# Four graph layers on one core: scores from upper and lower operand parts, and a layer norm folded into the product behind it

## The reference, cut to what matters

```python
# L0: two hypergraph convolutions with relu and a layer norm between them
h = relu(hypergraph_conv(x, adj, W1, b1))          # conv(x) = Dn * H @ (Be * (H.T @ (x @ W.T))) + b, H = (adj != 0)
h = layer_norm(h, gamma, beta)                     # (h - mu) * rsqrt(var + eps) * gamma + beta, over 512 channels
y = hypergraph_conv(h, adj, W2, b2) + x
# L1: transition matrix from exp(leaky_relu(si + sj)) * A, row-normed, then two hops
H = sum(Xk @ Wk[k] + bk[k] for k in range(3));  Xk = transition @ Xk     # out = relu(H)
# L2: eight heads of 32 channels
Xp = X @ Wp[h] + bp[h];  Xc = Xp @ C[h].T
attn = tanh(A * (Xc @ Xp.T));  Xh = attn @ Xp      # out = relu(Xh)
# L3
out = relu((a @ x) @ kernel) * mask
```

## Time and profile before

| | |
|---|---|
| median of 3 runs | 1648.58 us (1648.41 to 1649.86) |
| the profiled execution | 1649.85 us, its span 1648.0 us |
| TensorE busy | 1486.1 us (90%), 9850 products |
| VectorE, ScalarE, GpSimd busy | 1146.0 us (70%), 908.8 us (55%), 284.7 us (17%) |
| mean granted TensorE clock | 0.978 of full |

### The profile page before, as it was taken

How to read it: one execution, slowest core, us unless ns; L and a number is a source line. 1 busy time by engine, 2 the same in 40 slices (tenths; PEclk the granted TensorE clock), 3 DMA queues, 4 the chain that set the end, 5 groups by cost and what they waited for, 6 DMA issues and landing times.

```text
span 1648.0 us, 26778 instructions
## 1 busy us (share of the span) xinstructions
PE 1486.1 (90%) x9850; PEld 1085.8 (66%) x9850; DVE 1146.0 (70%) x2522; ACT 908.8 (55%) x1517; POOL 284.7 (17%) x348
## 2 busy tenths in 40 slices
PE   5688888899899999999999999999999999998986
PEld 4676666667666676766667676666767666676633
DVE  6564766758678686777868677786867778676663
ACT  3424555365565546556554655656465565646564
POOL 3111020202112030210303021030302103120001
PEclk9788999999999999999999999999999999999998
DMA  7010111112120211212021121202112121110021
...
DMA packets 58550, 92.17 MB, mean 56 GB/s; under 512 B 4288, under 2 KB 23296, under 8 KB 58496
## 3 DMA queue, kind: packets, MB, share of 16 engines
...
...
## 4 chain that ended last, share of the span: by engine, by line
PE 55%; issue 20%; DVE 16%; ACT 6%; POOL 2%; DMA 1%; SPq 0%; DVEq 0%; ACTq 0%; POOLq 0%
PE ring_f L1299 33%; PE ring_b L1299 9%; PE ring_b L1569 6%; PE pv_acc L1585 3%; DVE att L1133 3%; DVE bns L928 3%; PE ring_f L1468 2%; POOL rstd L489 2%; DVE rows L1030 2%; ACT hf L568 1%; DVE uz L952 1%; ACT rows L606 1%; DVE m L957 1%; DVE xc_s L952 1%; PE ring_f L1435 1%
## 5 line engine op out<-in xcount | busy, mean ns | idle before, releaser
L1133 DVE TENSOR_TENSOR att<-ring_b,at 128x1024 f32<-128x1024 f32 x256 | 307.2, 1219 | 77.1 <-PE ring_b L1569 69.7
L710 ACT ACTIVATE att<-att 128x1024 f32<-128x1024 f32 x256 | 265.1, 1054 | 136.2 <-DVE att L1133 135.2
L489 POOL TENSOR_TENSOR rstd<-var,mhalf 128x4 f32<-128x4 f32 x80 | 81.3, 1017 | 769.6 <-DVE var L943 769.6
L1299 PE MATMUL ring_f<-w,uz 128*128 128x256 f32 (+1 forms) x896 | 188.9, 333 | 2.3 <-DVE uz L952 1.7
L1299 PE MATMUL ring_f<-m,tr_h 128*128 128x256 f32 x1024 | 190.4, 287 | 0.0
L1299 PEld LDWEIGHTS ring_f<-m,tr_h 128*128 128x128 f32 x1024 | 158.9, 191 | 32.8 <-issue 32.1
L1299 PEld LDWEIGHTS ring_f<-w,uz 128*128 128x128 f32 x896 | 152.0, 192 | 29.8 <-DVE uz L952 12.2
L1585 PE MATMUL pv_acc<-att,xp_n 128*32 128x512 f32 x1024 | 138.5, 617 | 33.9 <-ACT att L710 26.8
L1569 PE MATMUL ring_b<-xc_t,xp_t 32*128 32x512 f32 x1024 | 147.6, 646 | 20.9 <-DVE att L1133 11.7
L1299 PE MATMUL ring_f<-m,inc_n 128*128 128x256 f32 x1024 | 132.2, 288 | 17.8 <-POOL m L493 16.3
L1299 PEld LDWEIGHTS ring_f<-m,inc_n 128*128 128x128 f32 x1024 | 127.0, 195 | 30.6 <-issue 18.7
...
## 6 DMA issues: line engine op xcount, KB each, us to landing
...
```

The lines of the kernel that those rows point to most:

```text
L489: pool.tensor_tensor(rstd[k][:], var[k][:], mhalf[:], ALU.pow).then_inc(rstd_made[k].sem, 1)
L710: act.activation(v, v, ACT.Tanh).then_inc(tanh_made.sem, 1)
L1133: dve.tensor_tensor(att[:, u % 2, 2 * half:2 * half + 2], ring_b[half][:], at[:, u % NT].unsqueeze(1).broadcast_to([P, 2, N]), ALU.mult).t ...
L1299: ins = pe.matmul(dst, lhsT, rhs, start=(first and n == 0), stop=(last and n == len(pairs) - 1), skip_group_check=True)
```

## The change

Five things, and new order lists on all five queues.

- Scores: `xp_t` and `xc_t` are each kept as an upper and a lower `fp32r` part. The new step `k_split` makes xp's (two operations of VectorE on 1024 columns), a new `k_xc` on VectorE xc's lower part. `k_scores` issues three rounds of four heads.
- The norm of z: `f_z` and its offset are gone. `f_zT` transposes the relu's output. `f_xw` scales rows by rstd on its way out of PSUM (`scaled`, `scaled_low` with `rstd[Z]`), and the mean and beta come in through a six-row product of `stat_t[0:6]` with `rowz[0:6]`, issued with the last part of `f_xw` instead of the first.
- The new step `f_stat` makes those six rows: five small operations on VectorE, four transposes of six columns into a ring bank, one copy on ScalarE.
- To make room, `xp_t` now lies in `hb`, and `xc_s` (with `ax_s`) in `tr_l`. `k_h2` waits for `xc_full`, `xn_full` and `xp_split` of the graph before, `f_tt` for `xp_full` and `o_full`.
- Set-up makes `rowz` instead of the first row of `rowb`.

```diff
-        xp_t = sb("xp_t", [P, 2, N])
-        xc_t = sb("xc_t", [P, 2, N])
-        xc_s = sb("xc_s", [P, 2, 2 * N], F32R)
+        xp_t = hb[:].rearrange("p t d -> p (t d)").rearrange("p (c n) -> p c n", c=2)
+        xp_s = sb("xp_s", [P, 2, 2, N], F32R)
+        xc_t = sb("xc_t", [P, 2, 2, N], F32R)
+        xc_s = tr_l[:].rearrange("p t n -> p (t n)").rearrange("p (a n) -> p a n", a=2)
...
-            def f_z(g, i):
-                if i == 0 and not seen(g, 1):
-                    set_up_w2()
-                normed(g, rows, rows, Z, i, ACT.Identity)
+            def f_stat(g):
+                act.wait_ge(stat_full.sem, stat_full.after(g, 1))
...
+                copy(stat_t[0:6], bank_of(ST, 0)[0:6], stat_copied)
...
-                copy(m1[:, 0, 2 * k:2 * k + 2].rearrange("p t d -> p (t d)"), bank_of(XW, k)[:], xw_hi)
+                scaled(k, bank_of(XW, k), rstd[Z], lambda t: m1[:, 0, t], xw_hi)
...
+            def f_stat(g):
+
+                cols = stat[:].rearrange("p t (a k) -> p a t k", a=2)
+                dve.wait_ge(rstd_made[Z].sem, rstd_made[Z].after(g, 1))
...
+                dve.tensor_scalar(pair[:, 0], sums[Z][:, :, 0], -0.5, None, ALU.mult)
+                c_stat.link(dve.tensor_tensor(pair[:, 1], var[Z][:], rstd[Z][:], ALU.mult))
+                here(c_stat, g)
+                dve.tensor_copy(cols[:, :, :, 0], pair[:])
+                c_stat.link(dve.tensor_copy(cols[:, :, :, 1], pair[:]))
+                here(c_stat, g)
+                dve.tensor_tensor(cols[:, :, :, 2], pair[:], cols[:, :, :, 0].bitcast(F32), ALU.subtract)\
+                   .then_inc(stat_made.sem, 1)
...
-                low(v[:, 1], bank_of(XW, k)[:], v[:, 0], xw_lo)
+                scaled_low(k, bank_of(XW, k), rstd[Z], lambda t: m1[:, 1, t], lambda t: m1[:, 0, t], xw_lo)
...
+            def k_split(g, part):
+                if part == 0:
...
+                    dve.wait_ge(xp_made.sem, xp_made.after(g, 2))
+                    dve.tensor_copy(xp_s[:, 0], xp_t).then_inc(xp_split.sem, 1)
+                else:
+                    dve.wait_ge(xp_split.sem, xp_split.after(g, 1))
+                    low(xp_s[:, 1], xp_t, xp_s[:, 0], xp_split)
+
+            def k_xc(g):
+                dve.wait_ge(xc_made.sem, xc_made.after(g, 1))
+                low(xc_t[:, 1], ring_b[0][:], xc_t[:, 0], xc_lo)
...
-                        pe.wait_ge(h_made[Z].sem, h_made[Z].after(g, i + 1))
+                        pe.wait_ge(relu_made.sem, relu_made.after(g, i + 1))
...
-                    pairs = [(sel[:], rowb[:, 0])] if ks[0] == 0 else []
+                    pairs = [(stat_t[0:6, i * P:(i + 1) * P], rowz[0:6])] if ks[-1] == HT_ - 1 else []
...
+            def f_stat(g):
+                pe.wait_ge(stat_made.sem, stat_made.after(g, 1))
+                ps = bank(g, ST, 0)
+                for i in range(NT):
+                    ins = pe.transpose(ps[0:6, i * P:(i + 1) * P], stat[:, i].bitcast(F32), ident[:])
+                ins.then_inc(stat_full.sem, 1)
...
-                for h in range(4):
-                    head = slice(h * KH, (h + 1) * KH)
-                    ins = pe.matmul(ring_b[h // 2][:, h % 2], xp_t[head, part, t * P:(t + 1) * P], xc_t[head, part],
-                                    start=True, stop=True, skip_group_check=True)
-                    if h % 2 == 1:
-                        ins.then_inc(scored.sem, 1)
+                for n, (p, c) in enumerate(((0, 0), (0, 1), (1, 0))):
+                    for h in range(4):
+                        head = slice(h * KH, (h + 1) * KH)
+                        ins = pe.matmul(ring_b[h // 2][:, h % 2], xp_s[head, p, part, t * P:(t + 1) * P],
+                                        xc_t[head, c, part], start=(n == 0), stop=(n == 2), skip_group_check=True)
+                        if n == 2 and h % 2 == 1:
+                            ins.then_inc(scored.sem, 1)
```

The lists of `turn`, for SP, TensorE and the part of VectorE's that the prediction speaks of (ScalarE's and GpSimd's are reordered in the same way):

```diff
 SP
-                    (0, next_x), (2, next_at), (0, next_wrow), (4, store), (2, next_at2), (0, next_adj),
+                    (0, next_x), (2, next_at), (4, store), (3, next_at2), (0, next_adj), (0, next_wrow),
                     (0, next_adjt),
 TensorE
-                    (0, f_m, 0), (0, f_m, 1), (2, k_attend, 2), (2, k_scores, 4), (0, f_u, 0), (0, f_u, 1),
-                    (2, k_attend, 3), (2, k_scores, 5), (0, f_conv1, 0), (0, f_conv1, 1), (0, f_conv1, 2),
-                    (0, f_conv1, 3), (2, k_attend, 4), (2, k_scores, 6), (2, k_attend, 5), (2, k_scores, 7),
-                    (0, f_zT, 0), (0, f_zT, 1), (1, k_hT), (0, f_zT, 2), (0, f_zT, 3), (0, f_xw, 0), (0, f_xw, 1),
-                    (0, f_xw, 2), (0, f_xw, 3), (2, k_attend, 6), (0, f_m2, 0), (0, f_m2, 1), (2, k_outT, 0),
-                    (2, k_attend, 7), (0, f_y, 0), (2, k_outT, 1), (0, f_y, 1), (1, k_xp, 0), (1, k_xp, 1),
-                    (1, k_xn, 0), (1, k_xc, 0), (0, f_hT, 0), (0, f_hT, 1), (1, k_xc, 1), (1, k_xn, 1), (0, f_sj),
-                    (0, f_q, 0), (0, f_q, 1), (2, k_ax, 0, 0), (0, f_q, 2), (0, f_q, 3), (2, k_ax, 0, 1),
-                    (2, k_ax, 1, 0), (2, k_ax, 1, 1), (2, k_out, 0), (2, k_out, 1), (0, f_tt, 0), (0, f_tt, 1),
-                    (0, f_tt, 2), (1, k_scores, 0), (0, f_tt, 3), (0, f_r1), (1, k_scores, 1), (0, f_r, 0),
-                    (1, k_attend, 0), (0, f_r, 1), (1, k_scores, 2), (0, f_x1), (1, k_attend, 1), (1, k_scores, 3),
-                    (0, f_x2, 0), (0, f_x2, 1),
+                    (0, f_m, 0), (2, k_scores, 3), (1, f_x2, 1), (2, k_attend, 2), (0, f_m, 1), (2, k_scores, 4),
+                    (0, f_u, 0), (2, k_attend, 3), (0, f_u, 1), (2, k_scores, 5), (0, f_conv1, 0), (0, f_conv1, 1),
+                    (0, f_conv1, 2), (0, f_conv1, 3), (2, k_attend, 4), (2, k_scores, 6), (0, f_zT, 0),
+                    (0, f_zT, 1), (2, k_attend, 5), (0, f_zT, 2), (0, f_zT, 3), (0, f_xw, 0), (0, f_xw, 1),
+                    (0, f_stat), (2, k_scores, 7), (0, f_xw, 2), (0, f_xw, 3), (2, k_attend, 6), (0, f_m2, 0),
+                    (0, f_m2, 1), (1, k_hT), (2, k_outT, 0), (0, f_y, 0), (2, k_attend, 7), (0, f_y, 1),
+                    (2, k_outT, 1), (1, k_xp, 0), (1, k_xp, 1), (1, k_xc, 0), (1, k_xc, 1), (1, k_xn, 0),
+                    (0, f_hT, 0), (0, f_hT, 1), (1, k_xn, 1), (0, f_sj), (0, f_q, 0), (0, f_q, 1), (2, k_ax, 0, 0),
+                    (0, f_q, 2), (0, f_q, 3), (2, k_ax, 0, 1), (2, k_ax, 1, 0), (2, k_ax, 1, 1), (2, k_out, 0),
+                    (2, k_out, 1), (0, f_tt, 0), (0, f_tt, 1), (0, f_tt, 2), (1, k_scores, 0), (0, f_tt, 3),
+                    (0, f_r1), (0, f_r, 0), (1, k_scores, 1), (0, f_r, 1), (0, f_x1), (1, k_attend, 0),
+                    (1, k_scores, 2), (1, k_attend, 1), (0, f_x2, 0),
 VectorE (the new one from conv1 on, then from the start of the list)
+                    (0, f_conv1, 0), (0, f_conv1, 1),
+                    (2, k_unit, 5, 1), (0, f_conv1, 2), (0, bn, 1, 0), (0, f_conv1, 3), (1, offset, 3),
+                    (0, bn, 1, 1), (0, bn, 1, 2), (0, bn, 1, 3), (0, f_zT, 0), (0, f_zT, 1), (0, variance, 1),
+                    (0, f_zT, 2), (0, f_zT, 3), (0, f_stat), (2, k_unit, 6, 0), (2, k_unit, 6, 1),
+                    (2, k_unit, 7, 0), (0, f_xw, 0), (0, f_xw, 1), (2, k_unit, 7, 1), (0, f_m2, 0), (2, k_outT, 0),
+                    (0, f_m2, 1), (1, k_hT), (0, f_y, 0), (0, f_y, 1), (2, k_outT, 1), (0, bn, 2, 0),
+                    (0, bn, 2, 1), (0, bn, 2, 2), (0, bn, 2, 3), (2, bn, 4, 0), (0, variance, 2), (2, bn, 4, 1),
+                    (2, bn, 4, 2),
+                    (0, bn, 0, 0), (1, offset, 2), (3, bn, 4, 3), (3, variance, 4), (3, offset, 4), (1, f_hT, 0),
+                    (1, f_hT, 1), (2, k_xc), (2, k_split, 0), (1, f_q, 0), (1, f_q, 1), (2, k_split, 1),
+                    (0, bn, 0, 1), (1, f_max, 0), (1, f_mask, 0), (1, f_q, 2), (1, f_max, 1), (1, f_q, 3),
+                    (1, f_mask, 1), (1, f_max, 2), (3, k_ax, 0), (1, f_max, 3), (1, f_mask, 2), (0, bn, 0, 2),
+                    (3, k_ax, 1), (3, k_mask), (1, f_mask, 3), (1, f_sums), (0, bn, 0, 3), (1, f_trans, 0),
+                    (1, f_trans, 1), (1, f_trans, 2), (1, f_trans, 3), (1, f_tt, 0), (1, f_tt, 1), (1, f_tt, 2),
+                    (1, f_tt, 3), (0, variance, 0), (2, k_unit, 0, 0), (0, offset, 0), (0, f_H), (2, k_unit, 0, 1),
```

More of the change, by code:

```diff
@@ new lines, in _ @@
+                (2, f_xw, 0), (2, f_stat), (0, k_scores, 7), (2, f_xw, 1), (2, f_xw, 2), (2, f_xw, 3),
+                (0, k_attend, 6), (0, k_attend, 7), (2, f_m2, 0), (2, f_m2, 1), (0, k_outT, 0), (0, k_outT, 1),
+                (1, k_hT), (2, f_y, 0), (2, f_y, 1), (1, k_xp, 0), (1, k_xp, 1), (1, k_xc, 0), (1, k_xc, 1),
+                (1, k_xn, 0), (1, k_xn, 1), (2, f_hT, 0), (2, f_hT, 1), (2, f_q, 0), (2, f_q, 1), (2, f_sj),
+                (2, f_q, 2), (2, f_q, 3), (0, k_ax, 0, 0), (0, k_ax, 0, 1), (0, k_ax, 1, 0), (0, k_ax, 1, 1),
@@ new lines, in _ @@
```

(10 more changed lines are left out.)

704 lines of the change are left out of this document (357 added, 347 removed).

## The result

The kernel after takes 1604.15 us, median of 4 runs (1603.98 to 1604.42), against 1649.22 of the kernel before (4 runs, 1648.41 to 1650.51): ratio 0.9725, 95% interval 0.9712 to 0.9737. The direction was right, the size was not.

The account below looks back on a forecast made before the run. TensorE, busy 90% of the span, was taken as the bound. 13 turns at -1.0 us, -4 for graphs 0 and 1 and -0.5 at the end took 1649.85 profiled to 1632.3, the median 1.3 lower: 1631 us, range 1618 to 1645.

Parts of the forecast that it names:

- A scores unit, 0.90 us: Scores on TensorE: three overlapping rounds take 0.90 us a unit for 1.07, gaining 0.17 a unit, 1.4 a turn.
- the two rivals on that, 1.12 and 3.0 us: Scores units: weight loads not hidden, 1.12 us, 1654 in all (chance 0.06); heads in single file, about 1850 (0.03).
- Row products change the shape: Six-row products in `f_xw` 2 and 3: each was taken to change TensorE's array shape in and out, 0.2 us a change.
- six rows change no shape: Rival on the six-row products: six changes fewer, -1.2 us a turn, 1615 us; chance 0.12.
- Idle time in A, -2.45 us: From conv1's end to `k_attend` 6: all 2.45 us of TensorE's idle time a turn go.
- the VectorE rival: From conv1's end to `k_attend` 6: VectorE holds TensorE, idle time returns before `k_scores` 7, 1663 us; chance 0.20.
- A in sum, -0.7 us: From conv1's end to `k_attend` 6, a turn: scores -0.35, shape changes +1.7, f_stat +0.4, idle time -2.45.
- B and C, +0.5: From `k_attend` 6 to `f_tt`: +0.5 us a turn, range 0 to 1.5, with 1.2 of waiting before `k_xp`.
- D, -0.8: From `f_tt` to the end of the next conv1, TensorE full: scores -1.0, shape change +0.2 us a turn.
- Graphs 0 and 1, -4 us: The start: graph 0's wait of 1.56 us for z at `f_zT`, both graphs' transposes and scores, together -4 us.
- The end: The kernel's last units: ten give 0.17 us each, the last graph's split takes 1.2 back, -0.5 in all.
- The clock: TensorE's granted clock in a turn: taken as full, with no term of its own in the sum.

Follow-up runs that it names:

- new_order_f32: The kernel after with its scores put back to four float32 products a unit, split steps still running: 1619.76 us, ratio 0.9820.
- rows_together: The kernel after with the four six-row products issued one behind another, right behind scores unit 7: 1588.13 us, ratio 0.9627.
- rows_128: The kernel after with the six-row products padded to 128 rows: 1583.83 us, ratio 0.9598.
- fold_new: The kernel after with float32 scores and the split steps taken off VectorE: 1623.90 us, ratio 0.9847.
- order_only: The kernel before, norm of z and float32 scores kept, in the order of the kernel after: 1710.84 us, ratio 1.0367.
- the fold alone: The kernel before with only z's norm folded into the W2 product, old order with f_stat put in: 1734.41 us, ratio 1.0494.

## Why the prediction was wrong

**A scores unit, 0.90 us.** Right: 0.92 and 0.84. The weights are hidden (the unit's twelve loads lie within 0.54 us of its start at 880.81) and the heads run side by side; the two rivals on that, 1.12 and 3.0 us, are out. The Trainium skill (TensorE: Matmul & The Clock Gate, "Part 3: Packing small matmuls") lets a weight load overlap running products only when their row groups differ, and beside that names a free background buffer as a case of its own; the trace disagrees with the first, for loads of one row group are hidden here. In the whole kernel the split gave 15.6 us where 1.4 us a turn would be 22: the forecast took 0.17 for each unit, and only six of eight give it (new_order_f32).

**Row products change the shape.** Right, each at 0.49 us; rows_together and rows_128 show it from both sides. The rival "six rows change no shape" would have come nearer to the measured time, and for a wrong reason.

**Idle time in A, -2.45 us.** Right: none is left. The followed queues held, and the VectorE rival is out (no idle ahead of `k_scores` 7; fold_new).

**A in sum, -0.7 us.** Too small by 0.7. Its length fell by 2.26, of which `k_hT`'s 0.87 went to B, so by 1.39. TensorE's work in A, `k_hT` aside, grew by 1.1 us (12.88 to 13.94) and not by 1.75. The mis-sized term is that of the changes of shape: 1.7 were counted for nine of them, and the W2 product with its rows grew by 1.36 (821.09 to 827.53 before, 6.44; 884.59 to 893.76 after, less f_stat and the scores unit, 7.80). rows_128, which takes them away, gives 1.26 a turn. The eight changes around the rows were 0.19 each, as forecast, but the stream between them got a little shorter. And the row products cause only seven of the nine; the other two come from the list, which puts `k_attend` 5 between the transposes of z, and show no cost. (By this count the rival "six rows change no shape" should take off seven changes, not six: 1613 us.) The transposes of z fell by 0.23 (2.10 to 1.87), f_stat cost 0.53 for 0.4, and some 0.2 are the ends of groups that a wait had laid bare.

**B and C, +0.5; D, -0.8.** Measured +0.3 and -0.9, with the waits of 1.4 and 1.2 in the forecast places; 0.8 for xp_t and 0.3 for hf are gone, and 0.6 for uz is new. A turn: -1.96 instead of -1.0, or about 12 us over the kernel.

**Graphs 0 and 1, -4 us. This is the step that failed most.** I priced only `f_zT`'s first wait and the scores there, and let the steady rate begin at 313 us. The kernel was 10.8 us ahead at graph 3 (307.9 to 297.1), and gained 14.7 more in the next three turns, where -1.0 a turn gave 3. Together 25.5 instead of 7. The start's lists were read only for that one wait. What the runs put there: order_only stands at graph 5 at 505.7 us, the kernel before at 505.1, the new order with the fold at 482.8 (float32 scores) and 481.6 (split). So neither the order alone nor the scores but the order with the fold shortened the start (the fold alone stands at 518.9), by less idle time (14 us) and more clock (7 us). The sum priced one wait there, that for z. What the order takes away is another, the waits for the gates and tanh of the first graphs' attention, 13.0 us in the kernel before and 1.3 after; for it the forecast has nothing beyond the steady turn's 1.5. Which of the start's many moves did it was not tried. The end is off too, by less: from graph 15 on the kernel after gained 2.8 us, where the last turn and the end were to give 1.5.

**The clock.** The sum took it as full, since the earlier trace rows show 1.00 in a steady turn. That was right for these turns. For the start it was a missing term, 7 us, and in the neighbouring orders it is 2 to 3 us a turn.
